# Row scaling of the first edge sweep moved to VectorE; the coupled sweep on five slots, its VectorE inputs partly read from PSUM

## What is computed

```python
x = _layernorm(x + _L0_gnn_ref(x, edge_index, edge_attr_4, edge_attr_32, W1, b1, W2, b2, ...))   # "weighted0"
x = _layernorm(x + _L1_gnn_ref(x, edge_index, edge_weight1, edge_attr_3, edge_attr_5, W))          # "coupled"
x = _layernorm(x + _L2_gnn_ref(...))                                                              # two convolutions
x = _layernorm(x + _L3_gnn_ref(...))                                                              # "weighted3"
# L0: w = (relu(edge_feat @ W1 + b1) @ W2 + b2) per edge, 4 paths of 8x8; the message is w times
#     (source row x spherical harmonics); the row scaled by harmonic 0 is one of its inputs
# L1: for each edge and each (le, ln, lo): einsum('ijk,ei,emj->emk', CG, sh[le], feats[ln]), then segment_sum
```

## Time and profile before

| | us |
|---|---|
| median of 3 runs (18817.78 to 18853.27) | 18837.07 |
| the profiled execution, its own time | 18865.37 |
| its span, first to last instruction | 18863.6 |
| first gather to last gather, first sweep | 57.2 to 4473.2 |
| the same, coupled sweep | 4672.4 to 8944.6 |
| the same, last sweep | 14687.0 to 18675.0 |

### The profile page before, as it was taken

How to read it: one execution, slowest core, us unless ns; L and a number is a source line. 1 busy time by engine, 2 the same in 40 slices (tenths; PEclk the granted TensorE clock), 3 DMA queues, 4 the chain that set the end, 5 groups by cost and what they waited for, 6 DMA issues and landing times. The chain is left out here.

```text
span 18863.6 us, 319178 instructions
## 1 busy us (share of the span) xinstructions
PE 14294.0 (76%) x90270; PEld 10545.9 (56%) x90270; DVE 13979.9 (74%) x35607; ACT 4058.3 (22%) x9245; POOL 9929.0 (53%) x9721
## 2 busy tenths in 40 slices
PE   8999999998666666666433337776777899999998
PEld 5666666665666666666322235555555555555555
DVE  7787788875333333333899999995999899999996
ACT  2332333332000000000100014443444222222222
POOL 6666666763777777777122210000000677777774
PEclk7777777876555555555555569997999999999998
DMA  1111111111111111111000003331333111111111
GB/s 34 25 25 25 25 25 25 26 25 17 16 16 16 16 16 16 16 16 16 8 1 1 1 32 132 134 133 63 132 134 116 19 18 18 18 18 18 18 18 15
DMA packets 997582, 680.36 MB, mean 36 GB/s; under 512 B 744566, under 2 KB 912467, under 8 KB 997044
## 3 DMA queue, kind: packets, MB, share of 16 engines
q1 hardware_dynamic: 694830, 524.39, 9.5%
q0 software_dynamic: 302720, 155.60, 5.9%
HBM read 669.41 MB, written 9.60 MB: 36 GB/s over the span
## 5 line engine op out<-in xcount | busy, mean ns | idle before, releaser
L526 PE MATMUL weighted_weights_ps<-weighted_w_out,weighted_hidden 128*128 128x256 f32 x12600 | 4127.7, 457 | 530.9 <-DVE weighted_to_s L665 478.6
L734 PE MATMUL coupled_win<-coupled_onehot,coupled_prod 128*125 128x64 f32 x12560 | 2763.8, 418 | 1533.6 <-DVE coupled_prod L770 1533.6
L356 POOL DMA_INDIRECT coupled_rows<-x_after_weighted,coupled_idx x3140 | 3307.2, 1053 | 1164.1 <-issue 954.8
L526 PEld LDWEIGHTS weighted_weights_ps<-weighted_w_out,weighted_hidden 128*128 128x128 f32 x12600 | 2451.6, 215 | 2539.9 <-issue 1698.0
L356 POOL DMA_INDIRECT weighted_rows<-in_x,weighted_idx x3140 | 3068.7, 977 | 1402.9 <-issue 920.0
L734 PEld LDWEIGHTS coupled_win<-coupled_onehot,coupled_prod 128*125 128x125 f32 x12560 | 2678.9, 329 | 1618.5 <-issue 834.8
L356 POOL DMA_INDIRECT weighted_rows<-x_after_convolved,weighted_idx x3140 | 3031.2, 965 | 1043.6 <-issue 940.9
L660 DVE TENSOR_TENSOR weighted_v_v<-weighted_weights_ps,weighted_scaled 128x320 f32<-128x320 f32 x3768 | 1964.5, 576 | 885.3 <-ACT weighted_scaled L587 885.3
L1198 DVE TENSOR_SCALAR cells_to_dst<-from,cells_current 128x224 bf16<-128x224 bf16 x12500 | 2389.7, 273 | 17.9
L1154 PE MATMUL cells_sum_ps<-cells_to_dst,cells_rows 128*96 128x224 bf16 x12500 | 1698.7, 267 | 691.6 <-DVE cells_to_dst L1198 691.6
L559 PEld LDWEIGHTS weighted_win_ps<-weighted_onehot,weighted_prod 128*128 128x128 f32 x12560 | 1833.4, 215 | 100.9
(11 more groups left out here) (203 smaller groups left out, 14930.0 us busy)
## 6 DMA issues: line engine op xcount, KB each, us to landing
cells_src<-cell_sources SPq DMA_DIRECT2D x500, 800.0 KB, 4.1
weighted_feat<-in_ef SPq DMA_DIRECT2D x635, 80.0 KB
weighted_rows<-in_x,weighted_idx POOLq DMA_INDIRECT x3140
coupled_rows<-x_after_weighted,coupled_idx POOLq DMA_INDIRECT x3140, 2.4
weighted_rows<-x_after_convolved,weighted_idx POOLq DMA_INDIRECT x3140
weighted_idx<-in_src_blocks SPq DMA_DIRECT2D x1264, 2.5 KB
weighted_sh<-in_sh SPq DMA_DIRECT2D x1264, 10.0 KB
coupled_sh<-in_sh SPq DMA_DIRECT2D x632, 22.5 KB, 1.7
```

Of the source, the lines that this page charges most:

```text
L356: pool.indirect_dma_start(rows[s][:, t, :], None, table, bass.IndirectOffsetOnAxis(ap=idx[s][:, t:t + 1].bitcast(U32), axis=0))\
L526: mm = pe.matmul(banks[bank][:, t * WPATHS:(t + 1) * WPATHS], hidden[slot][:, t * P:(t + 1) * P], w_out[:, :], start=True, stop=True)
L734: mm = pe.matmul(win_ps[s % 2][0:OCH, c * WINDOW:(c + 1) * WINDOW], prod[s][:, t, c * OCH:(c + 1) * OCH], onehot[s][:, t, :], start=(t == ...
```

## The change

1. The constants `DEEP = 5`, `LAG = 4`, `ROUNDS = 125`: the coupled sweep has five slots, 125 rounds of 5 and so 625 blocks instead of 628. The weighted sweeps keep four slots and 628 blocks.
2. The first weighted sweep: `scale_rows` is gone from ACT, and DVE's one instruction for it is no longer under `if deep`.
3. The coupled sweep has five PSUM windows instead of two. PE no longer waits on `summed`; block n-4's window is added after the messages of block n. The four windows that are left are added at the end of the pass. The five windows are zeroed at the start.
4. In the coupled sweep the column numbers `iota` lie in PSUM. ACT copies the harmonics of each block (128 x 45) from SBUF into one PSUM buffer `harm`, and DVE reads them there. ACT may overwrite `harm` when DVE has finished the messages of the block before (`msg_ready`, which starts at 1 so that the first copy may go), and DVE waits for `harm_ready`.
5. SP and POOL do for five slots what they did for four, written out in the function.

```diff
+DEEP = 5
+LAG = 4
+ROUNDS = REAL_BLOCKS // DEEP
...
-                def scale_rows(g, s):
-                    act.wait_ge(gathered[s], g * (16 * TILES) + 16 * TILES)
-                    act.wait_ge(loaded[s], g * 32 + 32)
-                    act.wait_ge(w_used, g * SLOTS + s + 1)
-                    for t in range(TILES):
-                        last = nc.scalar.activation(scaled_pair[s % 2][:, t, MUL:], rows[s][:, t, :], ACT.Copy,
-                                                    scale=sh[s][:, t, 0:1])
-                    last.then_inc(rows_scaled, 1)
...
-                        if not deep:
-                            scale_rows(g, s)
                         block_act(g * SLOTS + s + 3, (s + 3) % SLOTS)
...
-                            if deep:
-                                dve.tensor_tensor(scaled[:, :, MUL:], x[:, :, :],
-                                                  h[:, :, 0:1].broadcast_to([P, TILES, FEAT]), ALU.mult)\
-                                    .then_inc(rows_scaled, 1)
+                            dve.tensor_tensor(scaled[:, :, MUL:], x[:, :, :],
+                                              h[:, :, 0:1].broadcast_to([P, TILES, FEAT]), ALU.mult)\
+                               .then_inc(rows_scaled, 1)
...
-        iota, base_f, base = sb("iota", [P, WINDOW]), sb("base_f", [1, BLOCKS + SLOTS]), sb("base", [1, BLOCKS + SLOTS], I32)
-        win_ps = [ctx.enter_context(nc.psum_tensor(f"coupled_win{b}", [P, 512], F32)) for b in range(2)]
+        iota = ctx.enter_context(nc.psum_tensor("coupled_iota", [P, 512], F32))[:, 0:WINDOW]
+        harm = ctx.enter_context(nc.psum_tensor("coupled_harm", [P, 512], F32))
+        base_f, base = sb("base_f", [1, LAG + REAL_BLOCKS]), sb("base", [1, LAG + REAL_BLOCKS], I32)
+        win_ps = [ctx.enter_context(nc.psum_tensor(f"coupled_win{b}", [P, 512], F32)) for b in range(DEEP)]
...
+                        for s in range(DEEP):
+                            sp.wait_ge(msg_ready, (p * ROUNDS + i) * DEEP + s + 2)
+                            fill(s, i * DEEP + (DEEP + s))
...
-                        if s == 0:
-                            pe.wait_ge(summed, n + 1)
-                        else:
-                            pe.wait_ge(summed, n)
-                        pe.wait_ge(msg_ready, n + 1)
+                pe.sem_inc(spread, LAG)
+                pe.wait_ge(ones, ONES)
+                with pe.Fori(0, passes * ROUNDS, 1) as g:
+                    for s in range(DEEP):
+                        pe.wait_ge(msg_ready, g * DEEP + s + 2)
                         for c in range(2):
                             for t in range(TILES):
-                                mm = pe.matmul(win_ps[s % 2][0:OCH, c * WINDOW:(c + 1) * WINDOW],
+                                mm = pe.matmul(win_ps[s][0:OCH, c * WINDOW:(c + 1) * WINDOW],
...
+            @block.scalar
+            def _(act):
+                passes = Turns(act, k).passes
+                act.sem_inc(msg_ready, 1)
+                with act.Fori(0, passes * ROUNDS, 1) as g:
+                    for s in range(DEEP):
+                        act.wait_ge(loaded[s], g * 32 + 32)
+                        act.wait_ge(msg_ready, g * DEEP + s + 1)
+                        nc.scalar.activation(harm[:, 0:TILES * HARM], sh[s][:, :, :].rearrange("p t c -> p (t c)"), ACT.Copy)\
+                          .then_inc(harm_ready, 1)
...
-                def add_window(n, s, at):
-                    dve.wait_ge(summed, n + 1)
-                    dve.wait_ge(spread, n + 1)
+                passes = Turns(dve, k).passes
+
+                def add_window(spread_to, adds, s, at):
+                    dve.wait_ge(spread, spread_to)
+                    dve.wait_ge(summed, adds + 1)
                     dst = k["acc"][0:OCH, :, bass.ds(at, WINDOW)]
-                    dve.tensor_tensor(dst, dst, win_ps[s % 2][0:OCH, 0:2 * WINDOW].rearrange("p (c w) -> p c w", c=2),
+                    dve.tensor_tensor(dst, dst, win_ps[s][0:OCH, 0:2 * WINDOW].rearrange("p (c w) -> p c w", c=2),
                                       ALU.add).then_inc(summed, 1)
...
+                        for s in range(DEEP):
+                            n = g * DEEP + s
+                            x, h = rows[s], harm[:, 0:TILES * HARM].rearrange("p (t c) -> p t c", t=TILES)
+                            win.one_hot(onehot[s], i * DEEP + s)
                             dve.wait_ge(gathered[s], g * (16 * TILES) + 16 * TILES)
-                            dve.wait_ge(loaded[s], g * 32 + 32)
+                            dve.wait_ge(harm_ready, n + 1)
                             dve.tensor_tensor(
                                 prod[s][:, :, 0:4 * FEAT].rearrange("p t (c f) -> p t c f", c=4),
                                 h[:, :, 0:4][:, :, :, None].broadcast_to([P, TILES, 4, FEAT]),
...
-                            if s > 0:
-                                add_window(n - 1, s - 1, bases[s - 1])
-                        add_window(g * SLOTS + (SLOTS - 1), SLOTS - 1, bases[SLOTS - 1])
+                            if s == 0:
+                                bases = win.bases(i * DEEP, DEEP)
+                            add_window(n + 1, n + p * LAG, (s - LAG) % DEEP, bases[s])
+                    last = win.bases(REAL_BLOCKS, LAG)
+                    for j in range(LAG):
+                        add_window((p + 1) * REAL_BLOCKS + j + 1, (p + 1) * REAL_BLOCKS + p * LAG + j,
+                                   (j - LAG) % DEEP, last[j])
```

57 lines of the change are left out of this document (32 added, 25 removed).

## The result

The changed kernel takes **18090.08 us** (median of 4 runs, 18056.99 to 18140.02) against 18845.17 us for the kernel before (4 runs, 18817.78 to 18874.83). The ratio is 0.9598 with a 95% interval of 0.9579 to 0.9617. That is 755 us less; 718 was forecast, and the predicted 18119 us lies 29 us above the median. The profiled execution took 18071.57 us, its span is 18069.8; the span before was 18863.6, so 793.8 us are to be accounted for in the traces.

The account below looks back on a forecast made before the run. POOL's gathers were taken to bound the coupled sweep, PE with a loss at full clock the first. Coupled -368 and first -350 make -718 us, from 18837 to 18119 us; range 18020 to 18400.

Parts of the forecast that it names:

- rival A: Whole kernel: both the first and the coupled sweep gain as forecast, range 18020 to 18250 us; chance 0.78.
- part 6: First sweep: row scaling on DVE instead of ACT removes PE's waits and may hold the clock longer; -350 us.
- Part 1 and 5: Coupled sweep: three blocks fewer, -19 us, and a fifth slot that shortens POOL's wait at the start, -6 us.
- Part 2: Coupled sweep: products and one-hot matrix read one input from PSUM, so gathers are no longer lengthened; -343 us.
- Parts 3 and 4: Coupled sweep: ACT's copy of harmonics, and five windows added four blocks late, both off POOL's path; 0 each.
- longest gather would be near 960 ns: Coupled sweep sign: maximum indirect DMA near 960 ns, with the mean falling from 1053 to about 945.
- PE's wait for `to_s` is below 100 us: First sweep sign: PE's wait for DVE's `to_s`, 310.0 us before, falls below 100.
- B: First sweep: DVE takes ACT's place as limit, PE waits as before, only the coupled gain remains, 18469 us; chance 0.13.
- POOL's slot wait: First sweep sign: POOL's wait for slots that come free late, 427.3 us before, falls below 150.
- The upper bound of 427: First sweep: the gain can't exceed 427 us, because then POOL never waits for a slot.
- D: First sweep falls to the lower clock, about 0.70 mean to cancel the coupled gain; kernel slower than before; chance 0.03.
- The last sweep: Control sign: it still spans 3988 us within 5; otherwise something outside the argument has moved.

Follow-up runs that it names:

- g1: f3, but first sweep: ACT scales rows, one block of activations earlier; coupled sweep: all inputs from SBUF, no copy; 18453.29 us against 18818.43 for the kernel before.
- f1: Kernel before with long turns (twelve turns written out in each loop body of the edge sweeps); 18822.76 us against 18794.23 for the kernel before.
- e3: Changed kernel with only the coupled sweep's column numbers back in SBUF, under the slow passing condition; 22163.21 us against 22361.35 for the kernel before.
- f3: Changed kernel with twelve turns written out in each loop body of the edge sweeps; 18088.19 us, ratio 0.9628 to the kernel before.
- e5: Changed kernel with five spare ACT instructions per block in the first sweep, unread, under the slow passing condition; 22030.74 us.

## Why the prediction was right, and where it was not

**The forecast** of 18119 us, the range and the sign held, and rival A is what happened. Its two terms are not equally good, and that the time came within 29 us is partly luck: against the profiled execution, from whose rows it was worked out, the 18147 us were 75 too high, mostly the 80 us of part 6, and the two profiled executions happened to lie on opposite sides of their medians.

**Part 1 and 5** (three blocks fewer, fifth slot): forecast -25. The start wait fell from 8.70 to 1.17 us, 15 gathers are gone, and g1 against f1 gives -17 for both, in which g1's gathers were also 4 ns longer (1044 and 1040), some 12 us. Right within these.

**Part 2** (PSUM): forecast -343. The lengthened gathers were 343 us and are 2955.5 - 3125 x 0.944 = 5.5 now, and g1 gives 312 us for the PSUM inputs alone on another chip. Right in mechanism and size. The instructions cost the same from either memory, as taken. e3 and the trace of g1 add that the products carry nearly all of it. By the inferred note of the Trainium skill (SBUF — State Buffer, Who interferes with whom), that `tensor_tensor` holds up no writing of descriptors, PSUM would have brought nothing and the sweep would be 343 us longer; with this note the trace disagrees. The same section also has it that a VectorE instruction with two SBUF inputs contends with a GpSimd instruction that reads SBUF, which the prediction left out. The gathers take their indices (`coupled_idx`) from SBUF, and with that rule the trace agrees: 1053 ns beside products with two SBUF inputs, 946 with one. Which access of the gather is held up, no run shows.

**Parts 3 and 4** (copy, late windows): 0 each. ACT's copy took 212 ns, the list of waits of the sweep has none of DVE for it, and none of PE or DVE for a window. Right. The claim that the longest gather would be near 960 ns was off by little: 997, near the start of the sweep and beside no product.

**Part 6** (row scaling) is the term that was mis-sized: -350 forecast, -430 measured (-362 in the pair on the other chip). The lateness was the right cause: DVE's wait for ACT went, and g1 gets most of the gain by curing the lateness alone. What failed is the way from there to the time.

- The prediction had the sweep run at 5.85 us a block at full clock, set by DVE and PE. In the mean POOL does not allow it: the changed kernel takes 1.27 us a gather at full clock and 1.26 at half, 6.35 us a block, and PE and DVE wait behind that.
- The sentence "PE's wait for `to_s` is below 100 us" failed: 334.6. I had priced the gain as the 310 us of these waits and a little clock. Their sum did not fall; other waits stand in their place. PE does the same matmuls in 481 us less, since the time at half clock fell from about 2031 to 1036 us. By my own test "if PE's wait stays near 310 us, it is B" the text pointed to the wrong case: the wait stayed, and it was not B, because now DVE waits for rows and PE for DVE behind that. The test that decides is POOL's slot wait, at 21.6 of 427.3, below the 150 that I had named.
- The upper bound of 427 was POOL's slot wait and left out the gathers. They fell by 40 us, although the added instruction reads two SBUF inputs; I had set this at 0 with a risk upwards. Why they fell is not shown; the place of DVE's instructions relative to the gathers has moved too. In the long-turn pair they fell by only 8 us.
- The clock was named as a bonus within part 6 and as a danger in D. In PE's account the whole gain came through it. D's mirror image, 0.87 instead of 0.70, was not on the list of rivals.

**The last sweep** was to stay within 5 us and took 9.3 more (3997.30); 8 of it are its gathers, 3031.19 to 3039.32. The prediction took such a shift as a sign of something outside the argument. The same code took 3995.8 us in f1, 4001.1 in f3 and 4015.5 in g1, all with long turns, so the sweep varies by more than 9 us between kernels; the cause is not shown.

## What to carry to other kernels

When POOL's gathers bound a loop, put one input of each long VectorE multiplication beside them into PSUM, with a copy on an idle engine if need be: here a copy of 212 ns a block and the column numbers in PSUM saved 312 us. When an engine's result is late, look first at what stands in front of it in its own order; moving it one block earlier gave 325 of 362 us here. And where the granted clock alternates, the waits of the bounding engine need not get shorter when it gains: read PE's busy time and clock beside it, and bound the gain by the next engine's idle time plus what its own instructions may lose.

## What was not expected of the hardware

- The lengthening of a gather depends on a tenth of a microsecond: 1.51 us when it starts 0.13 us behind the two-SBUF product, 0.94 when it starts 0.10 us ahead. All 592 gathers of the kernel before that started 0.05 to 0.35 us behind the first product ended 0.12 to 0.14 us behind the second. With one input in PSUM no gather of 3125 took over 997 ns.
- A passing condition made every kernel 17% slower (22.1 for 18.8 ms) while POOL's gathers were no slower (946 ns in the mean in both) and DVE's long product neither (812 ns, 825 in the normal condition). PE had waits of up to 13.2 us about once in each turn of a loop. The change was worth 94 us in it and 755 outside. What it was is open. A comparison is only as good as the kernel before that ran beside it.
- Still open: why the clock rises sooner in the first sweep now, how much of the gain there is the clock's and how much the rows' being in time, and what ACT's load without its lateness would cost (e5 was not repeated in the normal condition). A version with the scaling left on ACT one block earlier and PSUM inputs was not run; from g1's first sweep, 37 us longer than f3's, nothing speaks for it.
